# Mamba and mixture-of-experts block: the decays of batches 1 to 5 in SBUF in place of the scan's PSUM bank

## The reference

```python
delta = softplus(dt_raw @ dt_proj_w.T + dt_proj_b)
A = -jnp.exp(A_log)
dA = jnp.exp(jnp.einsum('bti,is->btis', delta, A))
dBu = jnp.einsum('bti,bts->btis', delta * u, B_ssm)
def step(h, inp):
    dA_t, dBu_t, C_t = inp
    h = dA_t * h + dBu_t
    y_t = jnp.einsum('bis,bs->bi', h, C_t)
    return (h, y_t)
```

## Time and profile before

| | us |
|---|---|
| median of 3 runs | 607.68 (607.37 to 607.71) |
| the profiled execution | 606.02 |
| its span | 604.2 |
| VectorE busy in it | 581.3 (96%) |
| TensorE busy in it | 535.1 (89%) |
| GpSimd busy in it | 489.8 (81%) |
| ScalarE busy in it | 465.9 (77%) |
| batches 1 to 5 in it (118.9 to 477.1) | 358.2 |
| granted TensorE clock, mean | 0.98 |

### The profile page before, as it was taken

How to read it: one execution, slowest core, us unless ns; L and a number is a source line. 1 busy time by engine, 2 the same in 40 slices (tenths; PEclk the granted TensorE clock), 3 DMA queues, 4 the chain that set the end, 5 groups by cost and what they waited for, 6 DMA issues and landing times.

```text
span 604.2 us, 11465 instructions
## 1 busy us (share of the span) xinstructions
PE 535.1 (89%) x3578; PEld 419.5 (69%) x3578; DVE 581.3 (96%) x841; ACT 465.9 (77%) x952; POOL 489.8 (81%) x383
## 2 busy tenths in 40 slices
PE   5899889898898998999989999899989697778887
PEld 2377766647787878877887778877777465656564
DVE  6999989989999999999999999999999998999997
ACT  3899696369957998579876798768995589969880
POOL 3793466479999899998999889998997967885784
PEclk9899798989999999999999999999999999989999
DMA  7320229625787887889768888778874455233374
GB/s 200 148 91 2 74 60 282 226 84 184 237 314 237 311 277 222 292 244 339 262 189 305 276 305 275 243 257 274 284 264 157 156 219 197 103 100 108 79 143 87
DMA packets 61038, 122.48 MB, mean 203 GB/s; under 512 B 8362, under 2 KB 41778, under 8 KB 53938
## 3 DMA queue, kind: packets, MB, share of 16 engines
q1 hardware_dynamic: 53826, 112.42, 55.1%
q0 software_dynamic: 6144, 9.00, 6.6%
q10 hardware_dynamic: 1008, 0.33, 0.3%
HBM read 112.25 MB, written 9.47 MB: 201 GB/s over the span
## 4 chain that ended last, share of the span: by engine, by line
POOL 34%; PE 26%; DVE 15%; issue 14%; ACT 10%; DMA 1%; ACTq 0%; DVEq 0%; POOLq 0%; SPq 0%
POOL dbu L996 18%; POOL xs L980 6%; DVE bank L1213 6%; DVE h_sb L1232 5%; PE bank L1507 4%; PE bank L1541 3%; PE bank L1672 3%; ACT dbu L570 3%; PE bank L1686 2%; PE bank L1556 2%; ACT da L542 2%; PE bank L1564 2%; PE bank L1680 2%; POOL delta L463 2%; POOL sp_m L448 2%
## 5 line engine op out<-in xcount | busy, mean ns | idle before, releaser
L996 POOL TENSOR_TENSOR dbu<-du,xn_all 128x1024 f32<-128x1024 f32 x86 | 203.6, 2368 | 22.3 <-DVE bank L1213 13.7
L1213 DVE TENSOR_TENSOR_SCAN bank<-bank,dbu 128x512 f32<-128x512 f32 x160 | 195.2, 1222 | 1.0 <-ACT bank L554 0.7
L1232 DVE TENSOR_TENSOR h_sb<-bank,xh_all 128x512 f32<-128x512 f32 x230 | 152.5, 677 | 1.0
L1507 PE MATMUL bank<-id_sb,h_sb 128*128 128x128 f32 x992 | 132.5, 277 | 11.8 <-DVE h_sb L1232 9.3
L554 ACT ACTIVATE bank<-delta,a_sb 128x512 f32<-128x512 f32 x170 | 117.1, 691 | 27.5 <-DVE h_sb L1232 22.8
L1507 PEld LDWEIGHTS bank<-id_sb,h_sb 128*128 128x128 f32 x992 | 112.5, 143 | 26.5 <-DVE h_sb L1232 14.5
L1213 DVE TENSOR_TENSOR_SCAN bank<-da,bank 128x512 f32<-128x512 f32 x82 | 96.1, 1213 | 4.0 <-PE bank L1468 3.2
L1672 PEld LDWEIGHTS bank<-wd_sb,hid 117*128 117x128 f32 (+1 forms) x432 | 55.4, 190 | 42.8 <-issue 26.3
L980 POOL DMA_INDIRECT xs<-xn_rows,src x72 | 70.4, 978 | 12.8 <-issue 9.5
L1672 PE MATMUL bank<-wd_sb,hid 117*128 117x128 f32 (+1 forms) x432 | 62.9, 281 | 17.9 <-ACT xT L769 17.9
L570 ACT ACTIVATE dbu<-du_t,bc_sb 128x256 f32<-128x256 f32 x164 | 69.4, 497 | 5.8 <-PE bank L1468 3.4
(11 more groups left out here) (205 smaller groups left out, 906.8 us busy)
## 6 DMA issues: line engine op xcount, KB each, us to landing
xh_all<-b_rows SPq DMA_DIRECT2D x30, 1024.0 KB
xn_all<-b_rows SPq DMA_DIRECT2D x25, 1024.0 KB
wgu_sb<-in_w_gu SPq DMA_DIRECT2D x72, 352.0 KB, 4.2
wd_sb<-in_w_dn SPq DMA_DIRECT2D x72, 192.0 KB, 5.8
y_slots<-ys SPq DMA_DIRECT2D x72, 64.0 KB
xn_rows<-xn_all SPq DMA_DIRECT2D x2, 1040.0 KB, 10.2
out<-x_sb SPq DMA_DIRECT2D x7, 256.0 KB, 7.2
x_sb<-in_x SPq DMA_DIRECT2D x2, 640.0 KB, 5.9
```

What stands on the lines that cost most here:

```text
L996: nc.gpsimd.tensor_tensor(dbu[k % 2][:, :, :], du[b % 2][:, :, :], b_ring[c % 2][:, k % CH, :].unsqueeze(1).to_broadcast([P, NH, T]), ALU. ...
L1213: nc.vector.tensor_tensor_scan(to, da_of(n)[:, hf, :] if n in IN_SBUF else at, inp, 0.0, ALU.mult, ALU.add).then_inc(s["h_rdy"], 1)
L1232: nc.vector.tensor_tensor(h_sb[k % 2][:, hf, :], bank_of(b, 2 * k + hf)[:, :], row, ALU.mult).then_inc(s["p_rdy"], 1)
L1507: last = MM(HT[i][:, t % 2, hf * P:(hf + 1) * P], h_sb[k % 2][:, hf, t * P:(t + 1) * P], id_sb[:, :], is_transpose=True, start=(k == 0 and ...
```

## The change

For batches 1 to 5 `decay_bank` is replaced by `decay`: both halves of the decay of step n + 2 are made in step n and go to the ring of three SBUF buffers. `IN_SBUF` becomes all steps of batches 0 to 5 and the same steps of 6 and 7 as before. The scan reads its decay from `da` and its input from `dbu`, and writes the PSUM bank as before (or `h_sb`). It waits itself for the product that last read the bank. The first half of the first decay of batch 6 is still made into its bank, in the last step of batch 5.

```diff
-        IN_SBUF = [0] + BY_PE[:-(S - 2)] + [7 * S + 1] + BY_PE[-(S - 2):]
+        IN_SBUF = list(range(6 * S)) + [n for n in BY_PE if 6 * S <= n < 7 * S] + [7 * S + 1] + BY_PE[-(S - 2):]
...
-                if k + 2 < S:
-                    decay(k + 2)
-                elif k + 1 == S:
-                    decay_bank(S, 0)
+                decay(k + 2)
...
-                if b < 6:
-                    decay_bank(g, 1)
-                elif b == 6:
+                if b == 6:
...
-                elif k == 0:
+                elif b == 7 and k == 0:
                     decay(g + 1)
...
                 if b < 6:
-                    decay_bank(g + 1, 0)
+                    if g + 2 < 6 * S:
+                        decay(g + 2)
+                    elif k == S - 1:
+                        decay_bank(g + 1, 0)
...
                     wait(dve, "dbu_p", pooled_before(n) + 1)
                     inp = dbu[k % 2][:, hf, :]
+                    if n in IN_SBUF:
+                        bank_read(dve, freed(b, 2 * k + hf))
```

## The result

The changed kernel takes 752.19 us (median of 5 runs, 751.17 to 755.58), the kernel before 607.68 in the same comparison: a ratio of 1.2406 (95% interval 1.2385 to 1.2428). It is 144.5 us slower; the forecast was 747, with a range of 695 to 790. The profiled execution took 751.17 us, its span is 749.4.

The account below looks back on a forecast made before the run. VectorE and GpSimd, side by side and both nearly full, were taken to bound batches 1 to 5. Added: 86.1 (batches 2 to 4), 27.8 (1), 25.4 (5), together 139.3 on 606.02: 745.3, as median 747 us; range 695 to 790.

Parts of the forecast that it names:

- The new step: Batches 1 to 5: step from 4.37 to 5.71 us, or 6.64 with GpSimd's extra operation and a stopped load.
- The sum: Whole kernel: +139.3 us, all from batches 1 to 5; batches 0, 6 and 7 keep their code.
- By batch: Batches 2 to 4 +28.7 us each, batch 1 +27.8 (99.2 against 71.4), batch 5 +25.4 (95.3 against 69.9).
- The unknown that mattered: VectorE's scans reading two SBUF operands and GpSimd's tensor operations exclude each other for their whole length; likeliest case 65%, 747 us.
- The chain of waits alternates between scan and multiply: Expected sign in the new profile: the chain passes between VectorE's scan and GpSimd's multiply.
- ScalarE's order at no cost: ScalarE makes both decay halves late in the step, two states ahead; its extra 3.5 us of exps stays hidden.
- Nothing queued behind them is lengthened: ScalarE's queue: instructions behind the two moved decay exps take no longer; no cost.
- The one that waits goes next: VectorE and GpSimd: whichever waits during the other's operation gets its turn right after it, even between two GpSimd operations.
- Rival 1: GpSimd's indirect load is not stopped by the first scan; 48 steps save 0.69 us, total 714 us; 15%.
- Rival 2: A scan never waits, only GpSimd does; +92 us, total 700 us; 12%.
- Rival 3: Not slower: scans and multiplies don't meet; 0.7 us goes, total 607 us, or nothing happens; 4%.
- Rival 4: TensorE's clock becomes the limit below a granted 0.66; at 0.5 a batch takes 134 us, total 912 us; 4%.

Follow-up runs that it names:

- e3: Kernel before, with only the decay of half 0 of batches 1 to 5 in an SBUF buffer, ScalarE's order unchanged: 704.3 us.
- e4: Kernel before, with only the decay of half 1 of batches 1 to 5 in an SBUF buffer, ScalarE's order unchanged: 664.9 us.
- e6: Changed kernel with GpSimd's dbu multiply cut in two of 128x512, each waiting for its own half's scan: 749.8 us.
- e10: Changed kernel with GpSimd's indirect load moved behind the extra operation, the multiply left whole: 749.3 us.
- e11: Changed kernel with the dbu multiply cut in two and the indirect load moved behind the extra operation: 748.3 us.
- e5: Changed kernel with GpSimd's indirect load replaced by a plain DMA of 128 fixed rows from the same queue: 703.7 us.
- e1: Changed kernel with GpSimd's dbu multiply of batches 1 to 7 replaced by a constant fill: 665.2 us.
- e8: Kernel before with both halves' decays in SBUF, ScalarE's order unchanged, GpSimd's multiply and extra operations replaced by fills: 606.03 us, ratio 0.9998.

## Why the prediction was right, step by step

- *The new step.* 5.71 expected, 5.71 to 5.79 measured; 6.64 expected, 6.69 to 6.77 measured (6.05 to 7.37 around a `unit`, which moves time between neighbours: 7.36 + 6.06 = 2 x 6.71). In the step shown above the hand-overs are within 0.02 of the sum's: start of the multiply 0.08 after a scan, scan's end 1.10 after the multiply (1.08), load's end 0.77 after the scan (0.75).
- *The sum.* 139.3 against 145.15 (751.17 - 606.02), 5.9 short. Of these, 3 lie in batches 2 to 4, most of it the 0.07 in each of their eleven longer steps, and 2 in batch 1. Another 1.0 lies ahead of batch 1, which starts at 120.0 instead of 118.9. That is likely scatter and no cost of the change: e3 and e4, whose code for batch 0 is that of before, start it at 119.5 and 119.9.
- *By batch.* Batches 2 to 4: +28.7 expected, 102.0 - 72.3 = +29.7 measured. Batch 1: 99.2 expected, 101.2 measured, the largest miss of a batch; over half of it lies in its first five steps (28.2 for 27.05). Batch 5: 95.3 expected, 95.0 measured, in part by luck. Its steps without a load were put at 5.89 and take 5.66 to 5.78, since the extra operation ends 1.06 after the first scan and not its full 1.28; other steps are longer than said. `gate` and `unit` were hidden as said.
- *The unknown that mattered*, whether a scan waits for GpSimd, was bounded from the right rows: four records of other operations gave the rule for 160 scans. It was read from when they ended, not from how long they took.
- *One sign failed.* "The chain of waits alternates between scan and multiply" did not come true: GpSimd has 1% of it. A stop that counts as busy leaves no wait behind.
- *ScalarE's order at no cost* was right in the sum by luck, and wrong in its reason. "Nothing queued behind them is lengthened" failed: the tanh behind the exps is late, and that is worth 9 us once the cover (VectorE standing for the ports) is gone. The prediction named no cover there.
- *"The one that waits goes next"* was read from one record and held in the changed kernel, whose order gives GpSimd few back-to-back pairs. Rows 7 already spoke against it: there GpSimd stood for two scans in a row. As a general rule it fell in e6, e10 and e11, and the expectation of 710 with it.
- *Rival 1* (load not stopped) falls by the load's 1.71 and by e5. For the part that the Trainium skill (SBUF — State Buffer, Who interferes with whom) infers, that descriptor generation goes on beside a reader of two SBUF operands, the plain load in e5 agrees; the indirect load is longer all the same. *Rival 2* falls by scans of 2.57 and 2.20. The exclusive hold for the whole instruction, which the same page of the Trainium skill (section SBUF: two separate sides) states, agrees with both; that the one that starts first gets it does not, by the records, hold for the scans of 2.83 and 2.93 us in e4 and e1. *Rival 3* appears only when no tensor operation of GpSimd reads SBUF, in e8.
- *Rival 4.* The granted clock was 0.92 to 0.95 in batches 2 to 4, where it had been 1.00; TensorE is busy for 76% of batch 2 instead of 93%. It cost nothing there: VectorE has no idle time.

## What to carry to other kernels

Before an operand of VectorE moves from PSUM to SBUF, count the SBUF inputs of its instruction. Here the second one made a scan and the tensor operations of GpSimd that read SBUF exclude each other, for all but some 0.1 us of their length, and the cost was GpSimd's work that could no longer lie beside it. Look for it in durations and ends, since such a stop counts as busy and is missing from the waits and from the chain, and ask which instruction falls into the long one rather than how many there are. A cost that is hidden today (ScalarE's order, 9 us) comes out when the larger stop is removed.

## What was not expected of the hardware

- An indirect load of GpSimd stands while a scan reads two SBUF operands (0.98 to 1.71 us); a plain load from the same queue does not (0.57).
- Behind an indirect load GpSimd got the ports two or three times in a row although a scan waited (records of 3.4 to 4.7 us, 93 of 93 cases), and in e1 and e4 even ahead of a scan whose record starts first (16 cases). With plain loads it did so four times, and the same kernel is 75 us faster. The cause was not isolated further.
